# Decay chunks of 64 tokens instead of 128 in a two-direction Mamba-2 block, two chunks on the partitions, with new engine orders

## The reference, cut to what matters

```python
zxbcdt = x @ Win                                    # 256 -> 512 (z) + 640 (x, B, C) + 8 (dt)
xBC = silu(causal_conv4(xBC) + convb)               # per channel
dt = softplus(dt + dtb); A = -exp(Alog); dA = exp(dt * A)
h = dA_t * h + dt_t * outer(x_t, B_t)               # 8 heads, state 64 x 64 each
y_t = h @ C_t                                       # then + D * x, * silu(z), RMS norm, @ Wout
```

## Time and profile before

| | |
|---|---|
| median of 3 runs | 601.73 us (599.51 to 604.13) |
| the profiled execution | 603.06 us, of which 601.3 us from the first to the last instruction |
| busy, share of the span | TensorE 96%, ScalarE 88%, VectorE 79%, GpSimd 68% |
| granted TensorE clock | 0.994 of full |

### The profile page before, as it was taken

How to read it: one execution, slowest core, us unless ns; L and a number is a source line. 1 busy time by engine, 2 the same in 40 slices (tenths; PEclk the granted TensorE clock), 3 DMA queues, 4 the chain that set the end, 5 groups by cost and what they waited for, 6 DMA issues and landing times.

```text
span 601.3 us, 13719 instructions
## 1 busy us (share of the span) xinstructions
PE 577.1 (96%) x4320; PEld 464.5 (77%) x4320; DVE 476.6 (79%) x983; ACT 530.9 (88%) x1191; POOL 407.9 (68%) x427
## 2 busy tenths in 40 slices
PE   2998999999999999999999999999999999999996
PEld 1785788887888878887888878888788877888774
DVE  3689788986979779796889859797797968888663
ACT  4799998989989899998989899898999989898952
POOL 1016948797397965977487973979659774878932
PEclk9998999999999999999999999999999999999998
DMA  7464703436071621718034450717207180344601
GB/s 202 158 189 103 220 3 123 135 111 180 0 228 37 210 70 33 222 28 262 0 118 137 125 165 0 228 35 210 72 28 227 27 263 1 83 140 127 167 1 35
DMA packets 42009, 70.71 MB, mean 118 GB/s; under 512 B 6464, under 2 KB 29056, under 8 KB 41984
## 3 DMA queue, kind: packets, MB, share of 16 engines
q1 hardware_dynamic: 41984, 70.40, 39.4%
HBM read 59.37 MB, written 4.72 MB: 107 GB/s over the span
## 4 chain that ended last, share of the span: by engine, by line
PE 86%; ACT 6%; issue 3%; POOL 2%; DVE 1%; SPq 1%; DMA 1%; POOLq 0%; ACTq 0%; DVEq 0%
PE mi L612 18%; PE pj L478 12%; PE pj L479 10%; PE pj L480 10%; PE py L571 10%; PE py L589 4%; PE mi L678 4%; PE mi L558 4%; PE mi L538 3%; PE gm L545 1%; POOL xw L1856 1%; ACT L948 1%; PE mi L671 1%; PE mi L598 1%; PE mi L498 1%
## 5 line engine op out<-in xcount | busy, mean ns | idle before, releaser
L1372 DVE SCALAR_TENSOR_TENSOR xc<-pj,cw,xc 128x510 f32<-128x510 f32 (+2 forms) x240 | 173.4, 742 | 6.8 <-ACT xc L930 5.1
L963 ACT ACTIVATE bs<-bs,s_all 128x128 f32<-128x128 f32 x512 | 159.3, 391 | 0.0
L478 PE MATMUL pj<-xnt_hi,w_hi 128*128 128x512 f32 x288 | 128.0, 444 | 0.0
L1877 POOL TENSOR_TENSOR yg<-yg,sz 128x512 f32<-128x512 f32 x60 | 76.9, 1286 | 75.2 <-DVE yg L1418 75.2
L479 PE MATMUL pj<-xnt_lo,w_hi 128*128 128x512 f32 x288 | 114.6, 398 | 0.0
L480 PE MATMUL pj<-xnt_hi,w_lo 128*128 128x512 f32 x288 | 114.5, 398 | 0.0
L612 PE MATMUL mi<-wc,yg 128*128 128x256 f32 x480 | 111.8, 383 | 0.0
L612 PEld LDWEIGHTS mi<-wc,yg 128*128 128x128 f32 x480 | 88.8, 190 | 12.9 <-issue 1.8
L1856 POOL TENSOR_TENSOR xw<-xdt,w_end 128x512 f32<-128x512 f32 x48 | 49.4, 1043 | 54.6 <-ACT w_end L948 53.4
L1399 DVE TENSOR_TENSOR bs<-bs,gm 128x512 f32<-128x512 f32 x128 | 85.0, 675 | 0.2
L1384 DVE TENSOR_TENSOR xdt<-mi,dt 128x512 f32<-128x512 f32 x64 | 42.5, 686 | 45.4 <-PE mi L538 45.0
(11 more groups left out here) (152 smaller groups left out, 986.8 us busy)
## 6 DMA issues: line engine op xcount, KB each, us to landing
bs<-rows_dram SPq DMA_DIRECT2D x64, 512.0 KB, 5.4
es<-rows_dram SPq DMA_DIRECT2D x64, 192.0 KB, 4.8
cc<-bcm SPq DMA_DIRECT2D x32, 128.0 KB, 2.4
xres<-in_x SPq DMA_DIRECT2D x8, 512.0 KB, 3.6
out<-ot SPq DMA_DIRECT2D x32, 128.0 KB, 4.7
xin<-in_x SPq DMA_DIRECT2D x7, 512.0 KB, 3.6
cz<-bcm SPq DMA_DIRECT2D x16, 128.0 KB, 2.4
yg<-in_fwin SPq DMA_DIRECT2D x2, 320.0 KB, 3.4
```

Of the source, the lines that this page charges most:

```text
L478: pe.matmul(ps[:], hi(k), xnt_hi[:, k, :], start=(k == 0), stop=False)
L963: i = nc.scalar.activation(bs[:, h, Q * c:Q * c + Q], bs[:, h, Q * c:Q * c + Q], ACT.Relu, bias=s_all[:, d, 0, h, c:c + 1], scale=-1.0)
L1372: i = dve.scalar_tensor_tensor(xc[:, t, to], pj[bank][:, of], cw[:, d, t, KW - 1 - s:KW - s], xc[:, t, to], ALU.mult, ALU.add)
L1877: pool.tensor_tensor(yg[:, d, p, :], yg[:, d, p, :], sz[:, d, p, :], ALU.mult).then_inc(yg_ready, 1)
```

## The change

Chunks become 64 tokens long, so there are eight per batch (`NK`), and chunks 2c and 2c + 1 lie on the lower and the upper 64 partitions of what was chunk c. `bs` shrinks from 512 to 256 columns a head. There are seven entering states instead of three, and `xw` is made for all four token blocks. The orders of all five queues and the `mi` sequences are written anew. The core of the diff:

```diff
-START = [... "0S", "w6", "0ST", "w7", "w8", "1S", "0x0", "0bt", "1ST", "0x1", "0s0", "0x2", "0x3", "0s1", "0s2"]
+START = [... "0S", "0ST", "w7", "w8", "0x0", "0bt", "0x1", "0s0", "0s1", "1S", "0x2", "0x3", "0s2", "0s3", "0s4", "0s5", "0s6", "1ST"]
+LOOP = ["1x0", "1x1", "1bt", "1x2", "1x3", "a0", "a1", "1s0", "1s1", "1s2", "1s3", "0ss", "dtm", "0o0", "dtt", "1s4",
+        "1s5", "1s6", "0S", "0o1", "0ST", "0x0", "0x1", "0x2", "0x3", "0bt", "1ss", "0s0", "0s1", "0s2", "0s3",
+        "1o0", "1o1", "1S", "0s4", "0s5", "0s6", "1ST", "t0", "t1", "f0", "f1", "t2", "t3", "f2", "f3"]
...
 def repeat_heads(b, d, p):                      # SP
-    sp.dma_start(bs[:, 2 * p:2 * p + 2, :], rows_dram[d, 0, 2 * p:2 * p + 2, :].partition_broadcast(P))
+    for r in range(2):
+        sp.dma_start(bs[LANES[r], 2 * p:2 * p + 2].rearrange("p h c q -> p (h c) q"),
+                     rows_dram[d, 0, 2 * p:2 * p + 2].rearrange("h (c n) -> (h c) n", c=NC)[:, H * r:H * r + H]
+                     .partition_broadcast(HP)).then_inc(bs_loaded[p], 16)
...
 def sums(phase, it, b, d):                      # PE: one total for each of the two chunks of a block
-    pe.matmul(ps[:, NCH:2 * NCH], ones, av, start=True, stop=True).then_inc(full, 1)
+    for r in range(2):
+        mm = pe.matmul(ps[:, NCH * (r + 1):NCH * (r + 2)], which[:, r, :], av, start=True, stop=True)
...
 def scores(phase, it, b, d):                    # PE
     for c in range(NC):
-        mm = pe.matmul(gm[:, Q * c:Q * c + Q], bcm[:, d, Q * c:Q * c + Q], cz[:, Q * c:Q * c + Q], ...)
+        for r in range(2):
+            part = slice(Q * c + H * r, Q * c + H * r + H)
+            mm = pe.matmul(gm[LANES[r], H * c:H * c + H], bcm[0:NS, d, part], cc[0:NS, d, part], ...)
...
 def state(phase, it, b, d, j):                  # PE: two states from one block, each from 64 partitions
+    for n in (2 * j, 2 * j + 1):
+        if n < NK - 1:
+            rows = LANES[PIECE[d][n] % 2]
+            ps, full = misc(phase, it, f"{d}s{n}")
+            alone(pe)
+            for half in range(2):
+                mm = pe.matmul(ps[LANES[half], ...], btok[rows, c, :], heads[rows, :, MEMBERS[half], :], ...)
+            mm.then_inc(full, 1)
...
+def crossed(b, d, two, first):                  # PE: 16 matmuls, 64x64 weight, 64 columns, four quarters
+    for c in range(NC):
+        for i in range(2):
+            p = 2 * two + i
+            for half in range(2):
+                r = half ^ i ^ first
+                mm = pe.matmul(py[bank][LANES[half], piece], xdt[LANES[r], c, ...], bs[LANES[r], h, c, :], ...)
 def intra(b, d, two):                           # was: per p, 8 matmuls of 128x64 weight and 128 columns
+    crossed(b, d, two, True)
 def inter(phase, it, b, d, two):
+    pe.wait_ge(far_done, 4 * (2 * u + two + 1))
+    crossed(b, d, two, False)
     pe.wait_ge(c2_ready, 2 + KI * u + 2 * two + 2)
-    for j in range(NC - 1):                     # 3 x 4 matmuls of 128 columns
+    for j in range(NK - 1):                     # 7 x 4 matmuls of 64 columns
...
-def decay(b, d, h):     # ACT, per head: bs[:, h, :], 512 columns
+def decay(b, d, p):     # ACT, per pair: bs[:, 2p:2p+2], 512 columns
-def weights(phase, it, b, d, h):                # DVE, per head
+def weights(b, d, p):                           # DVE, per pair of heads, 512 columns
```

```diff
 def reversed_scan(...):   # x0 x1 project8 bt x2 x3 a0 a1, then
-    scores state0 state1 project(0) dt project(1) dtt project(2) squares mix0 mix1 project(3) state2 intra0 intra1
-    inter0 project(4) sums mix2 mix3 project(5) s_transposed intra2 intra3 inter1 project(6) project(7)
+    scores state0 project(0) state1 project(1) squares project(2) dt mix0 dtt project(3) mix1 project(4) state2
+    intra0 state3 project(5) inter0 sums mix2 mix3 intra1 s_transposed inter1 project(6) project(7)
 def forward_scan(...):
-    project8 x0 x1 project(0) x2 bt scores x3 squares project(1) state0 state1 project(2) mix0 mix1 intra0 state2
-    intra1 inter0 mix2 sums mix3 project(3) project(4) intra2 s_transposed intra3 inter1 t0 t1 project(5) f0 f1 ...
+    x0 x1 project8 x2 x3 project(0) bt squares scores state0 project(1) state1 project(2) mix0 mix1 mix2 sums mix3
+    project(3) state2 intra0 state3 project(4) s_transposed inter0 project(5) t0 t1 intra1 f0 f1 inter1 t2 ...
```

## The result

The changed kernel takes 643.5 us (639.5 to 645.8, four runs) against 602.9 before: a ratio of 1.067, with a 95% interval of 1.064 to 1.071. The forecast was 603, so the change is 7% slower where none was expected. The profiled execution of the changed kernel spans 641.8 us, 40.5 more than before.

The account below looks back on a forecast made before the run. TensorE, busy 96% of the span, was taken to bound the kernel. Its own work +1, new waits +3 and the ends -2 gave +2 us on the 601.7 us median, rounded down to 603 us; range 588 to 620.

Parts of the forecast that it names:

- The pace of TensorE: Quarter-array steps of 64x64 weights and 64 columns: limited to 0.056 to 0.06 us by load and stream, hand-out 0.018 a record.
- TensorE's own work, per turn: Loop turn of two scans: savings in matmuls offset by added states, sums and passages; +0.1 us a turn, +1 over 16 scans.
- Passages: TensorE's changes between array shapes: 18 a turn become 24, at 0.17 us each, +1.0 us a turn.
- New waits of TensorE, per turn: TensorE waiting in the loop for GpSimd's `xw` or at `squares`: 0.4 us a turn, bounds 0 and 1.5; +3 us.
- The two ends: First scan -2 us, bounds -3.3 and +2, from a standstill and half clock before `intra`; last scan 0.
- The DMAs of `bs`: Transfers of `bs`, halved in bytes and doubled in number, eight more on SP a turn: costed at nothing.
- Chain of the states: Rival, 618 us, chance 0.26: seven state links through TensorE, VectorE and GpSimd delay `inter` 1 us in each of 16 scans.
- Hand-out of records: Rival, 646 us, chance 0.06: short quarter steps handed out no faster than 0.0275 us a record, +5.4 us a turn.

Follow-up runs that it names:

- `double_intra`: Changed kernel with the diagonal-crossing half of `intra` issued twice, 32 more records in each of a turn's four blocks: 670.2 us, ratio 1.111.
- `merged`: Changed kernel with TensorE's order alone edited: `state0` and `state1` adjacent in both loop scans, second `intra` directly before second `inter`: 680.8 us, ratio 1.127.
- `dve_fill`: Changed kernel with VectorE's forward-scan order edited: both `wd` subtractions and one convolution before `feed` 0, another convolution before `feed` 1: 640.4 us, ratio 1.064.
- `chain_off_psum`: Changed kernel with `wd` subtractions reading one operand from PSUM, GpSimd's `decayed_state` left out and states not carried: 628.4 us, ratio 1.044.
- `after_one`: Changed kernel with one semaphore increment added behind each float32r projection matmul on TensorE: 662.6 us, ratio 1.100.
- `wd_psum`: Changed kernel with both `wd` subtractions right behind the copy of the sums, reading one operand from PSUM: 645.2 us, ratio 1.069.
- `ends`: Changed kernel with the last scan reordered: a projection between second and third `x_tokens`, two `mix` calls between `inter(., 0)` and `intra(., 1)`: 643.3 us, ratio 1.067.

## Why the prediction was wrong, step by step

- *The pace of TensorE* was right. Four records in 0.064 us by the starts, forecast 0.060 to 0.070, and 0.016 a record again from `double_intra`.
- *TensorE's own work, per turn.* Forecast +0.1 us. Measured turn less its waits: 70.3, forecast 70.3 on a turn that itself held 0.4 us of waits; so +0.5, within the bounds. (The bad ends of the terms add up to +3.1, not to the +4.1 that I wrote.) `sums` was mis-sized (0.66, not 0.45). `scores` with its exit lost 0.22, not 0.85, for 0.6 of it is waiting for `xw`.
- *Passages* were counted right, 24, at about the price taken: a clean `state` call, 0.58 us with its exit, adds 0.10 us ahead of it and 0.10 behind it, so 0.35 for the trip over its 0.43 of work. But they were read as pure cost; `merged` showed that what stands between them hides more than that.
- *New waits of TensorE, per turn*: this step failed. I took 0.4 us with a bound of 1.5; it was 2.9 more than before. I had named `squares` and the two `xw` (1.0 us of it), and missed the second state's bank, the `pj` bank behind the reversed `inter`, and the largest, the projection behind VectorE's queue. By `dve_fill`, 0.86 of the 2.9 is that largest one, and by `chain_off_psum` 0.1 to 1.0 is the chain with GpSimd's added work; for the rest the trace gives the place and no experiment the cause. I worked out GpSimd's order in detail and took VectorE's for granted because its busy time fell. The `wd` subtractions, which the diff moved from a PSUM operand to two in SBUF, weren't costed at all; with them VectorE's forecast 56.0 us was 57.7.
- *The two ends*: this step failed too. Forecast -2 us, bounds -3.3 and +2; measured +5.5 at the start and +12.0 behind the last mark, 8.9 of it in the last scan. The standstills before `intra` that I meant to see gone are gone, but another of 2.0 us with the same fall of the clock stands 13 us later. The gain of 2 us doesn't come without it either: `after_one`, which has none, is at +0.1 there, and TensorE now waits 1.0 us for `hst` before the first `inter`. In the last scan I took 0 for a chain that `chain_off_psum` prices at 4.2.
- *A term put at nothing.* The DMAs of `bs` at nothing: right, packets rose from 42,000 to 99,100, and no wait of TensorE names a DMA.
- *Missing*: no term and no rival was about the number of TensorE's instructions. The diff takes it from 1155 to 1797 a turn, and the forecast itself counted many of the added records.
- *The rivals.* "Chain of the states" (618) is a part of the truth. "Hand-out of records" (646) has nearly the measured time by another mechanism: its pace was refuted, and that its number fits is chance.

The sum by the runs, in the profiled execution: loop, six periods 20.2 us (2.9 of waits and 0.5 of work in each) and 2.7 for a code standstill; start 5.5, of which 5.4 a standstill at a fetch with its half clock (against `after_one`); end 12.0, of which 4.2 the chain and 3.1 the rest of the seventh turn. Some 5 us of the last scan are told by place only (half clock at `mix`, the `py` bank, `x_tokens` in a row) and not by an experiment.

## What to carry to other kernels

When the bounding engine gets more and smaller instructions, count them per loop trip: past a size the loop no longer stays loaded, and the price comes in standstills that no semaphore explains, in most of them with a slower clock behind. When a change rewrites the orders of all engines, cost the queues of the engines with slack as well as the full one: ask of every instruction ahead of a bank's release what it waits for, and whether both its operands lie in SBUF beside a busy GpSimd. And before removing a passage or a gap, ask which wait it hides: an experiment that clears one cause can hide its gain in another. And compare two runs stretch by stretch before crediting an edit with their difference: here the same start took from 71.2 to 77.3 us.

## What the runs showed of the hardware

- A VectorE `tensor_tensor` of 64x32 with both inputs in SBUF ends 0.07 us behind a GpSimd instruction that runs when it wants to start (it takes 0.20 us alone, up to 1.24 in the changed kernel and 1.53 in `dve_fill`); with one input in PSUM it took 0.20 to 0.21 in all 32 cases of `wd_psum`.
- TensorE stops 1.7 to 3.6 us in the middle of straight code or at the top of a loop when its instructions are fetched anew. Behind the one at 65 us the granted clock fell to 0.50 in six of the eight profiles that have it, and stayed at 1.00 in `dve_fill` and `ends`.
- A loop of TensorE of 1587 executed instructions stays in place, one of 1905 or 2019 doesn't, and one of 1797 is fetched again at none, one or two of its five returns.
- One semaphore increment of TensorE behind a 128x512 matmul is hidden; four in a row cost about 0.1 us each (starts 0.60 to 0.64 us apart).
- Quarter-array matmuls of 64x64 by 64 columns run at 0.016 us a record for 56 records without slowing down.
